# One comparison for four one-hot tiles in the carries between edge orders of a graph network

## The reference, cut to what matters

```python
h = x @ W.T
e = leaky_relu(h[src] @ a_src + h[dst] @ a_dst, ALPHA)
seg_max = segment_max(e, src)
exp_e = exp(e - seg_max[src])
denom = segment_sum(exp_e, src)
attention = exp_e / denom[src]
h_prime = segment_sum(attention[:, None] * h[src], dst)
```

## Time and profile before

| | us |
|---|---|
| median of 3 runs | 9635.66 (9634.32 to 9646.82) |
| the profiled execution | 9562.17 |
| its span, from the first to the last instruction | 9560.3 |
| first carry (`ps`), PE's matmuls | 261.2 busy, starting at 5300.8 |
| second carry (`pb`), PE's matmuls | 260.6 busy, starting at 5602.4 |

### The profile page before, as it was taken

One profiled execution on the slowest core, in us unless ns is written; L12 is line 12 of the kernel. 1 busy time (PEld: TensorE's weight loads), 2 busy tenths in 40 slices (PEclk: granted clock), 3 DMA queues, 4 the chain that ended last, 5 costly groups with the idle time before them and its releaser, 6 DMA issues. The chain is left out here.

```text
span 9560.3 us, 99896 instructions
## 1 busy us (share of the span) xinstructions
PE 5960.4 (62%) x15032; PEld 2923.7 (31%) x15032; DVE 6713.4 (70%) x20701; ACT 2831.8 (30%) x6861; POOL 4490.4 (47%) x4367
## 2 busy tenths in 40 slices
PE   0006999996999997776000889867869999800000
PEld 0002333332444444664000446723323333300000
DVE  2677888885666665887555898867869999877422
ACT  0002333331111112554333000134434444346300
POOL 1775555554555553554554000055556666313466
PEclk9998555555656665555555897578855555555555
DMA  4002334432222221111333002566633333322222
GB/s 146 1 1 44 56 56 56 56 56 50 47 47 47 46 47 28 36 37 44 85 88 80 5 4 67 150 109 130 128 67 74 72 74 73 81 89 110 79 82 78
DMA packets 937356, 627.70 MB, mean 66 GB/s; under 512 B 649081, under 2 KB 811542, under 8 KB 935760
## 3 DMA queue, kind: packets, MB, share of 16 engines
q1 hardware_dynamic: 580324, 305.65, 12.4%
q0 software_dynamic: 137984, 138.92, 11.8%
q10 hardware_dynamic: 218920, 181.82, 5.8%
HBM read 431.25 MB, written 228.04 MB: 69 GB/s over the span
## 5 line engine op out<-in xcount | busy, mean ns | idle before, releaser
L722 POOL DMA_INDIRECT a_xg<-t_XL,a_ix x784 | 785.5, 1002 | 668.3 <-issue 647.5
L722 POOL DMA_INDIRECT b_xg<-t_H,b_ix x784 | 783.3, 999 | 668.1 <-PE b_bank L932 379.6
L722 POOL DMA_INDIRECT g_xg<-t_D,g_ix x784 | 825.8, 1053 | 527.7 <-issue 227.4
L1762 POOL DMA_INDIRECT f_dg<-t_D,f_ix x392 | 383.9, 979 | 1291.1 <-DMA f_ix<-t_PSRC 1163.7
L1105 POOL DMA_INDIRECT t_RANK<-m_place,m_at x392 | 384.5, 981 | 415.0 <-DMA m_place<-t_POS 307.3
L1290 POOL DMA_INDIRECT l_d<-t_D,l_ix x392 | 370.8, 946 | 401.7 <-DVE l_xs L1306 234.1
L2177 POOL DMA_INDIRECT out<-o_y,o_ix x392 | 386.6, 986 | 230.9 <-issue 198.7
L1380 PE MATMUL pr_prow<-c_ident,pr_col 128*1 128x128 f32 x2 | 0.6, 394 | 786.0 <-DVE pr_col L1398 786.0
L445 POOL DMA_INDIRECT t_XL<-ix_pv,ix_si x392 | 407.9, 1041 | 160.0 <-issue 137.7
L760 DVE TENSOR_TENSOR b_zt<-b_xl,b_bank 128x512 f32<-128x512 f32 x98 | 67.4, 687 | 550.9 <-issue 210.2
L1339 ACT ACTIVATE l_hn<-l_xs,l_sm 128x64 f32<-128x64 f32 x784 | 265.0, 426 | 501.7 <-issue 259.6
(11 more groups left out here) (439 smaller groups left out, 17014.5 us busy)
## 6 DMA issues: line engine op xcount, KB each, us to landing
t_XL<-in_nodes ACTq DMA_DIRECT2D x10, 2578.1 KB
t_XSD<-a_xg SPq DMA_DIRECT2D x98, 256.0 KB
t_H<-a_oE ACTq DMA_DIRECT2D x98, 256.0 KB
l_xb<-t_XSD SPq DMA_DIRECT2D x49, 512.0 KB
f_rl<-t_REL SPq DMA_DIRECT2D x49, 512.0 KB
g_xb<-t_XSD SPq DMA_DIRECT2D x98, 256.0 KB
n_x<-in_x SPq DMA_DIRECT2D x39, 640.0 KB
out<-n_y ACTq DMA_DIRECT2D x39, 640.0 KB
```

What stands on the lines that cost most here:

```text
L722: nc.gpsimd.indirect_dma_start(xg[k][:, j, i, :], None, table, bass.IndirectOffsetOnAxis(ap=ix[k][:, i, j:j + 1], axis=0)).then_inc(s_g[k] ...
L1762: nc.gpsimd.indirect_dma_start(dg[k][:, u, j, :], None, T["D2"], bass.IndirectOffsetOnAxis(ap=ix[k][:, u, j:j + 1], axis=0)).then_inc(s_g[ ...
```

## The change

The narrow tiles of four columns are made by one instruction. `lhs` becomes two buffers of four tiles each (128 x 4 x 128), in place of four buffers of one. At each fourth column DVE issues one `tensor_tensor` with the operation is_equal over 128x512: one operand is `count[:, 0:128]`, repeated over the four tiles, the other is `part[:, c:c+4]`, each word repeated over 128 columns. Both repetitions are access patterns with a step of zero. The wide tiles, all waits, and PE's 392 matmuls are as they were, but for where a matmul's weights come from.

```diff
-        lhs = [m.sb(f"lhs{k}", [P, P]) for k in range(SL)]
+        G = 4
+        lhs = [m.sb(f"lhs{k}", [P, G, P]) for k in range(2)]
...
+            across = C["count"][:, 0:P].unsqueeze(1).to_broadcast([P, G, P])
             for c in range(EF):
                 k = c % SL
                 if c >= SL:
                     dve.wait_ge(s_mm, c - SL + 1)
-                v.tensor_scalar(lhs[k][:, :], C["count"][:, 0:P], part[:, c:c + 1], None, ALU.is_equal)
+                if c % G == 0:
+                    v.tensor_tensor(lhs[c // G % 2][:, :, :], across, bcast(part[:, c:c + G], P), ALU.is_equal)
                 v.tensor_scalar(rhs[k][:, :], C["count"][:, :], col[:, c:c + 1], value[:, c:c + 1],
                                 ALU.is_equal, ALU.mult).then_inc(s_hot, 1)
...
-                nc.tensor.matmul(sums[:, :], lhs[c % SL][:, :], rhs[c % SL][:, :], start=(c == 0), stop=(c == EF - 1)
+                nc.tensor.matmul(sums[:, :], lhs[c // G % 2][:, c % G, :], rhs[c % SL][:, :], start=(c == 0), stop=(c == EF - 1)
                                  ).then_inc(s_mm, 1)
```

## The result

The changed kernel takes 9750.58 us (median of 4 runs, 9742.96 to 9754.51), the kernel before 9637.83 (4 runs, 9634.32 to 9646.82). The ratio is 1.0115, 95% interval [1.0097, 1.0132]: 113 us slower. The forecast was 9636.5, and "slower" had been given a chance of 0.08.

The account below looks back on a forecast made before the run. The prediction took PE's own matmul pace to bound the carries. The profiled 9562.17 us plus 0.8 for later starts gave 9563.0; with 73.5 for the timed median over the profiled execution, 9636.5 us, range 9622 to 9656.

Parts of the forecast that it names:

- PE bounds the carry, by its own pace: In both carries PE's matmuls lead at 0.658 us a column; DVE has 0.06 us of slack in each column.
- The comparison, 0.60 us from start to start: DVE's 128x512 comparison takes 0.60 us per four columns, replacing four narrow tiles of 0.20 us each, 0.80 us.
- The late start, 0.40 us a carry: PE's first matmul in each carry starts 0.40 us later, as the first `rhs` does; +0.8 us for two carries.
- the +-1.2 us: PE's clock may rise earlier or later after the moved start of a carry: 0 on the mean, +-1.2 us for both.
- The waits: At each fourth column DVE waits for PE; its 1.08 us of work fits PE's remaining 1.81, so PE isn't starved.
- Rival 1: In the carries DVE, not PE, sets the pace and the change frees it: 4.7 us gained at most, 9631.8; chance 0.04.
- Rival 2: In the carries a slow comparison, from 1.03 us, makes DVE the bound; at 1.29 us +50 us, 9687; chance 0.05.
- Rivals 3 and 4: Narrow tiles give back less than 0.20 us: nothing, or 8 us, 9644; change runs as four comparisons: 9635.7; chance 0.03 each.
- nothing outside them changes: Outside the two carries the program keeps its time; a carry's loss or gain passes to the whole one for one.
- a program whose instructions lie elsewhere: Allowance for moved instructions, together with the three runs' 12.5 us spread: 0.04 on the fast side, 0.03 on the slow.

Follow-up runs that it names:

- two comparisons: Changed kernel without 96 of the 98 comparisons of each carry, plus 12 one-column DVE memsets; 9210.47 us, ratio 1.0004 to the kernel before.
- ten tiles: Changed kernel with each comparison made over ten tiles (128x1280, PE uses four), plus 76 one-column DVE memsets; 9277.58 us, ratio 1.0076 to the kernel before.
- N = 52: Kernel before plus 52 one-column DVE memsets ahead of a transfer wait in the second carry; 9666.61 us, ratio 1.0141 to the kernel before.
- N = 6: Changed kernel plus 6 one-column DVE memsets in the second carry; 9312.93 us, ratio 1.0120 to the kernel before.
- N = 40: Kernel before plus 40 one-column DVE memsets in the second carry; 9552.23 us, ratio 1.0014 to the kernel before.

## Why the prediction was wrong

- "PE bounds the carry, by its own pace": right, and now shown: less work on DVE does not shorten it (two comparisons: 260.6 us of PE's matmuls against 261.2), and more work lengthens it once DVE needs 2.98 us per four columns against PE's 2.63.
- The comparison, 0.60 us from start to start: 0.61. The rule that was weighed there, from VectorE: DVE Perf Modes of the Trainium skill (section "Why `tensor_tensor` can't do 2×_2P or 4×"), counts elements. By it the comparison would cost more than the four narrow tiles; the run has 0.61 us against 4 x 0.20 = 0.80, as the rows had.
- The late start, 0.40 us a carry: there to the digit. That the clock's earlier rise hid it in the first carry is luck, within the +-1.2 us that the prediction had left for both carries.
- The waits: at a fourth column DVE waits 0.17 us for PE, and PE never for DVE after the start. Right.
- Rival 1 (DVE sets the pace) is refuted by the run with two comparisons: 761 records of PE in 250 us, as before, where its pace of 0.326 us would give 767. Rival 2 did not occur; its mechanism and its price were confirmed by the ten tiles. Rivals 3 and 4 did not occur.
- The step that failed is a sentence of the first part, which put everything outside of the carries at nothing: "nothing outside them changes". DVE's instructions behind the carries are the same, but stand 588 places earlier. The text had named "a program whose instructions lie elsewhere" and left it a few hundredths as if it were noise of the measurement. It is a mechanism with a place, a condition and a price: two loops of 289 and 270 instructions, four blocks of 128 instead of three. In the bad places it costs 21 to 24 us in `relation_block` and 102 to 108 us in the third `gat_block` (741.1 and 744.4 against 720.2, 1411.4 against 1309.1 on one chip; 1390.5 against 1282.1 on the other). Together that is about 126 us in the kernel before with N = 52, whose ratio allows 114 to 157; the two profiles of the first comparison give 48 + 85 = 133, and its measured 113 us has an interval of 93 to 127.

What could have been read beforehand: that the page has a row of instruction packets on q14; that the built programs show how far everything behind a change moves on its engine, here by 588; and that two loops behind it are long. What the runs added is the rule: 588 is 76 over a multiple of 128, and the loops have a little more than 2 x 128 instructions, so that their placing counts. By the stretches that the expectations above name, 33 of 128 placings are bad for the loop of 289 and 15 for that of 270; the two loops stand so that 45 are bad for one or both. With this rule a blind chance for a loss of this kind is not 0.03 but about a third (an estimate; the edges of the stretches were not measured one by one). The size of a stall is shown by nothing in the trace of before.

The Trainium skill has a rule on it, which the prediction did not draw on: Runtime: NRT & Kernel Launch (section "Instruction fetch mechanics") says that an engine holds a small window of its program, refilled in blocks, and that a taken branch to a target outside of the window stalls until it is fetched. The stalls of 3 us after the jump agree, with two packets on q14 in the one shown. It gives 16 KiB blocks of 256 instructions, two at a time. For PE the size fits this trace: its 784 LDWEIGHTS and 784 MATMUL of the first carry go with 6 packets of 16 KB on q8. For DVE the runs decide otherwise: packets are of 8192 bytes, and starts of the loop of `relation_block` that are 128 apart in DVE's program modulo 256 behave alike (5212 in the changed kernel and 5852 in the kernel before with N = 52, 92 and 220 past a multiple of 256, both slow), which blocks of 256 would not give.

## What to carry to other kernels

An edit of straight-line code moves every later loop of that engine against the blocks in which its instructions are fetched. On DVE here, two loops of a little over two blocks began to stall in every turn with nothing in their code changed. Look at the count of instruction packets and at "issue" waits of the first operation of a loop before judging the edit itself, and try the edit again with a few cheap instructions ahead of the loop (here 16 one-column memsets under a wait, worth 1.1%). And a cheaper feeder buys nothing where the engine that is fed already runs at its own pace: find whose wait is there at the end of the stretch.

## What was not expected of the hardware

- DVE's instruction fetch: one packet of 8192 bytes per 128 instructions. In the first carry 784 instructions took 6 packets and in the changed kernel 490 took 4 (windows 5302 to 5562 and 5340 to 5600). PE's program is the same in both, and the packets on q8 stay at 6, so they are PE's:

```profile
q8 instruction: 6, 0.10, 0.1%
q14 instruction: 6, 0.05, 0.1%
```

```profile
q8 instruction: 6, 0.10, 0.2%
q14 instruction: 4, 0.03, 0.0%
```

- A loop that touches four such blocks is fetched anew in each turn, five packets at a time (113 - 14 = 99 for 20 turns); one that touches three is not fetched again. Loops of 211, 183 and 181 instructions elsewhere on DVE cannot touch four, and one of 259 stands so that it doesn't. That DVE holds four blocks, one of them fetched ahead, would explain it; this was not tested by itself, and the count of blocks that a loop touches is worked out from its length and place, not seen.
- The wait ahead of a turn's first operation depends on where the loop begins. In the third `gat_block` it is 3.2 us at 91 (63.2 us in 20 turns) and 5.2 at 97 (109.2 in 21); in `relation_block` 6.0 at 92 (54.2 in 9) and 4.3 at 80 (34.3 in 8). The stage becomes longer by about DVE's added stalls: in the third `gat_block` of the changed kernel the two groups have 63.2 + 22.6 - 7.7 = 78 us more, and the stage took 1403.8 - 1318.7 = 85 us more; with N = 6 it is 103 and 108 (against ten tiles, whose `g_zt` has 6.1). In `relation_block` part of them is absorbed: on one chip 31 and 50 us more of stalls made the stage 21 and 24 us longer (the kernel before with N = 40 and N = 52).
- An equality of two operands that both have a step of zero costs 692 ns over 128x512, as with one such operand, and 1487 ns over 128x1280, where a TENSOR_TENSOR of the kernel before (`n_y`, L2086) has 1488.
